# How the rows of graphs 1 to 3 are picked: by one-hot products on TensorE, or by transfers with an index

## What is computed

```python
x = x + tanh(g_xattn[0]) * xattn(ctx_512, layernorm(x))    # two gat layers, 8 heads of 32
x = x + tanh(g_ffn[0]) * ffn(layernorm(x))                 # top 2 of 8 experts
# gat layer: e = leaky_relu(a_self[i] + a_neigh[j]) - 1e10 * (1 - adj[i, j]); out = softmax(e) @ feat + b; elu
```

## Time and profile before

| | |
|---|---|
| time, median of 3 runs | 93.64 us (93.17 to 95.05) |
| time of the profiled execution | 93.16 us |
| its span, first to last instruction | 91.4 us |
| PE busy | 83.3 us (91%), 615 matmuls |
| DVE, ACT, POOL busy | 64.7, 55.2, 43.5 us |
| mean granted clock of PE | 0.996 |
| DMA | 5.44 MB; 386 to 405 GB/s from 6.9 to 13.7 us |

### The profile page before, as it was taken

One profiled execution on the slowest core, in us unless ns is written; L12 is line 12 of the kernel. 1 busy time (PEld: TensorE's weight loads), 2 busy tenths in 40 slices (PEclk: granted clock), 3 DMA queues, 4 the chain that ended last, 5 costly groups with the idle time before them and its releaser, 6 DMA issues.

```text
span 91.4 us, 1958 instructions
## 1 busy us (share of the span) xinstructions
PE 83.3 (91%) x615; PEld 78.1 (85%) x615; DVE 64.7 (71%) x202; ACT 55.2 (60%) x132; POOL 43.5 (48%) x95
## 2 busy tenths in 40 slices
PE   4959999989999999999999999999999999999800
PEld 4728888869899999989998999999999999999700
DVE  5887797857897609998599368795359767899520
ACT  1446888596695948398927799763366564433100
POOL 7970953698003999925900002885002988800000
PEclk9999999999999999999999999999999999999998
DMA  1999991000000000000000000030000030003021
GB/s 34 286 273 400 405 386 60 0 0 0 7 4 0 0 0 0 7 0 4 0 0 0 7 0 0 4 115 4 7 0 0 0 115 0 0 7 115 4 84 56
DMA packets 3339, 5.44 MB, mean 60 GB/s; under 512 B 474, under 2 KB 2748, under 8 KB 3068
## 3 DMA queue, kind: packets, MB, share of 16 engines
q1 hardware_dynamic: 3164, 5.00, 16.0%
q10 hardware_dynamic: 160, 0.26, 1.1%
HBM read 4.21 MB, written 1.05 MB: 58 GB/s over the span
## 4 chain that ended last, share of the span: by engine, by line
PE 59%; DVE 17%; DMA 6%; issue 6%; ACT 5%; DVEq 1%; POOL 1%; ACTq 1%
PE bank L734 6%; DMA ctx_sb<-in_ctx_t 6%; PE bank L735 6%; PE bank L739 6%; PE bank L896 6%; PE bank L781 5%; PE bank L872 5%; PE bank L783 5%; PE bank L782 5%; DVE hid_lo L1093 4%; PE bank L859 3%; PE bank L756 3%; DVE hid L1085 2%; PE bank L679 2%; DVE stat L990 2%
## 5 line engine op out<-in xcount | busy, mean ns | idle before, releaser
L1085 DVE TENSOR_TENSOR hid<-act_sb,bank 128x256 f32<-128x256 f32 x32 | 13.4, 418 | 10.9 <-PE bank L756 9.0
L518 ACT ACTIVATE act_sb<-bank,small_sb 128x256 f32<-128x256 f32 x32 | 15.1, 471 | 8.7 <-PE bank L739 8.4
L526 ACT CAST hid_hi<-hid 128x256 fp32r<-128x256 f32 x32 | 13.0, 405 | 10.7 <-DVE hid L1085 9.7
L781 PE MATMUL bank<-wdown_hi,hid_hi 128*128 128x256 f32 x64 | 18.4, 287 | 0.3 <-ACT hid_hi L526 0.3
L734 PE MATMUL bank<-xt_hi,wup_hi 128*128 128x256 f32 x64 | 18.0, 304 | 0.1
L783 PE MATMUL bank<-wdown_hi,hid_lo 128*128 128x256 f32 x64 | 18.1, 282 | 0.0
L782 PE MATMUL bank<-wdown_lo,hid_hi 128*128 128x256 f32 x64 | 18.0, 281 | 0.0
L735 PE MATMUL bank<-xt_hi,wup_lo 128*128 128x256 f32 x64 | 16.6, 281 | 0.0
L1093 DVE TENSOR_TENSOR hid_lo<-hid,hid_hi 128x256 fp32r<-128x256 f32 x32 | 13.4, 420 | 0.2
L739 PE MATMUL bank<-xt_lo,wup_hi 128*128 128x256 f32 x64 | 12.7, 280 | 0.0
L734 PEld LDWEIGHTS bank<-xt_hi,wup_hi 128*128 128x128 f32 x64 | 12.1, 189 | 0.5 <-ACT act_sb L518 0.3
(11 more groups left out here) (147 smaller groups left out, 180.6 us busy)
## 6 DMA issues: line engine op xcount, KB each, us to landing
x_sb<-in_x SPq DMA_DIRECT2D x4, 256.0 KB, 5.1
wup_sb<-in_wup SPq DMA_DIRECT2D x1, 1024.0 KB, 7.2
wdown_sb<-in_wdown SPq DMA_DIRECT2D x1, 1024.0 KB, 9.4
out<-out_sb SPq DMA_DIRECT2D x3, 256.0 KB, 2.2
check_sb<-in_check_w SPq DMA_DIRECT2D x1, 320.0 KB
w_sb<-in_w SPq DMA_DIRECT2D x1, 256.0 KB, 5.5
out<-out_sb SPq DMA_DIRECT2D x2, 128.0 KB, 2.5
ctx_sb<-in_ctx_t ACTq DMA_DIRECT2D x1, 192.0 KB, 5.6
```

The costliest lines, as they stand in the source:

```text
L518: nc.scalar.activation(act_out(n), bank[:, UP[n % 2], 0:N], ACT.Silu, bias=bup_sb[:, k % E:k % E + 1]).then_inc(silu_rdy, 1)
L526: nc.scalar.copy(hid_hi[:, n % HID_SLOTS, :], hid[:, n % 2, :]).then_inc(hid_hi_rdy, 1)
L781: nc.tensor.matmul(dst, hid_hi[:, n % HID_SLOTS, part], wdown_hi[:, e, :], start=False, stop=False, skip_group_check=True)
L1085: nc.vector.tensor_tensor(hid[:, n % 2, :], act_out(n), bank[:, PICK[n % 2], 0:N], ALU.mult).then_inc(hid_rdy, 1)
```

## The change

Graph 0 stays as it was. For graphs 1 to 3 the one-hot matrices, their transposes and squares and the products with z go. In their place:

- DVE writes for each row the number of its leader (`rows_leader`, `max_index`) into `leader`, 8 numbers a row, of which the first is used.
- SP stores `leader` of each graph to HBM, and later z of each graph. These six stores stand in SP's list behind all the loads.
- POOL (`leaders`) waits for the store and issues for each half graph a transfer that takes row leader(i) of the stored list into `leader2`: the leader of the leader. `fetch` takes row leader2(i) of the stored z into `rows`. Two transfers of 128 rows each for each graph: twelve in all. They stand among POOL's other work, `leaders(1)` ahead of `wup_part(0)`, `leaders(2)` ahead of `row_power(0)`.
- `gated` of graphs 1 to 3 waits for `rows_ld` and reads SBUF. On DVE `gated(1)` moves into step 0 of the expert loop, `gated(2)` to step 4, `gated(3)` to step 7. `wup_part(3)` on POOL moves ahead of `row_power(1)`.
- On PE `feat1(2, 1)` moves ahead of the transposes of graph 0. Some banks and the waits that guard them change.

```diff
-        onehot = sb("onehot", [P, NT, N], BF16)
-        onehot_t = sb("onehot_t", [P, B, C, N], BF16)
+        onehot = sb("onehot", [P, C, N], BF16)
+        onehot_t = sb("onehot_t", [P, C, N], BF16)
         source = sb("source", [P, C, N])
-        source_next = sb("source_next", [P, B - 1, C, N])
+        leader = sb("leader", [P, NT, 8], U32)
+        leader2 = sb("leader2", [P, NT, 8], U32)
+        rows = sb("rows", [P, B - 1, C, N])
+        leader_hbm = [nc.dram_tensor(f"leader_hbm{b}", [N, 8], U32) for b in range(1, B)]
...
+
+            for b in range(1, B):
+                sp.wait_ge(leader_rdy, C * b)
+                sp.dma_start(leader_hbm[b - 1][:].rearrange("(c p) k -> p c k", p=P), leader[:, pair(b), :]).then_inc(leader_st[b - 1], 16)
+            for b in range(1, B):
+                sp.wait_ge(z_rdy, b + 1)
+                sp.dma_start(z_hbm[b - 1][:].rearrange("(c p) d -> p c d", p=P), elu_exp[:, b, :, :]).then_inc(z_st[b - 1], 16)
...
-            def rows_onehot(b):
+            def leaders(b):
+                pool.wait_ge(leader_st[b - 1], 16)
                 for t in range(C * b, C * b + C):
-                    pool.wait_ge(top_rdy, t + 1)
-                    nc.gpsimd.tensor_scalar(onehot[:, t, :], x_sb[:, t, :], top[:, t, 0:1], None,
-                                            ALU.is_equal).then_inc(onehot2_rdy, 1)
+                    nc.gpsimd.indirect_dma_start(leader2[:, t, :], None, leader_hbm[b - 1][:],
+                                                 bass.IndirectOffsetOnAxis(leader[:, t, 0:1], 0)).then_inc(leader2_ld[b - 1], 16)
+
+            def fetch(b):
+                pool.wait_ge(leader2_ld[b - 1], 16 * C)
+                pool.wait_ge(z_st[b - 1], 16)
+                for t in range(C):
+                    nc.gpsimd.indirect_dma_start(rows[:, b - 1, t, :], None, z_hbm[b - 1][:],
+                                                 bass.IndirectOffsetOnAxis(leader2[:, C * b + t, 0:1], 0)).then_inc(rows_ld[b - 1], 16)
 
-            rows_onehot(1)
-            rows_onehot(2)
...
+            leaders(1)
             wup_part(0)
+            leaders(2)
             row_power(pool, 0, 0)
-            rows_onehot(3)
+            leaders(3)
             wup_part(1)
+            fetch(1)
             wup_part(2)
+            fetch(2)
+            wup_part(3)
             row_power(pool, 0, 1)
-            wup_part(3)
+            fetch(3)
             wdown_part(0)
             wdown_part(1)
             row_power(pool, 0, 2)
+            for b in range(1, B):
+                pool.wait_ge(rows_ld[b - 1], 16 * C)
...
-            turned(1)
...
-            source_copy(1)
...
-            source_copy(2)
...
-            act_experts(act, 0, {0: [lambda: source_copy(3)], 1: [lambda: wdown_part(0)],
+            act_experts(act, 0, {1: [lambda: wdown_part(0)],
                                  3: [lambda: wdown_part(1)], 5: [lambda: wdown_part(2)], 7: [lambda: wdown_part(3)]})
...
             if n == 1:
-                pe.wait_ge(z_rdy, B)
+                pe.wait_ge(z_rdy, 2)
...
-                pe.wait_ge(xa_rdy, C * (3 + nb))
+                pe.wait_ge(z_rdy, B - nb)
...
-            turn(0)
+            turn()
             feat1(0, 0)
             feat1(0, 1)
-            twice_part(0)
+            twice()
             feat0(3)
-            turn(1)
             feat1(1, 0)
-            gather(0)
-            twice_part(1)
+            gather()
             feat1(1, 1)
-            turn(2)
             feat1(2, 0)
-            twice_part(2)
+            feat1(2, 1)
             pe_xt(pe, 0, 0)
-            feat1(2, 1)
-            turn(3)
             feat1(3, 0)
             pe_gate(pe, 0, 0)
             feat1(3, 1)
-            twice_part(3)
-            gather(1)
-
-            pe_experts(pe, 0, {1: [lambda: gather(2)], 4: [lambda: gather(3)]})
+
+            pe_experts(pe, 0, {})
...
+            def rows_leader(b):
+
+                for t in range(C * b, C * b + C):
+                    dve.wait_ge(top_rdy, t + 1)
+                    nc.vector.max_index(leader[:, t, :], top[:, t, :], x_sb[:, t, :]).then_inc(leader_rdy, 1)
...
-                    dve.wait_ge(gather_mm, C + b)
-                    nc.vector.scalar_tensor_tensor(out=xa[:, pair(b), :], in0=both(GATHER[b][0]), scalar=gates[:, 0:1],
+                    dve.wait_ge(rows_ld[b - 1], 16 * C)
+                    nc.vector.scalar_tensor_tensor(out=xa[:, pair(b), :], in0=rows[:, b - 1, :, :], scalar=gates[:, 0:1],
                                                    in1=x_sb[:, pair(b), :], op0=ALU.mult, op1=ALU.add).then_inc(xa_rdy, C)
...
             elu0(0)
             rows_top(1)
+            rows_leader(1)
             elu0(1)
...
             elu1(0)
+            rows_leader(2)
+            elu0(3)
             rows_top(3)
-            elu0(3)
             gated(0)
             dve_stats(dve, 0, 0)
-            turned(2)
+            rows_leader(3)
...
-            turned(3)
...
-            gated(1)
-            dve_stats(dve, 0, 1)
...
-            dve_experts(dve, 0, {0: [lambda: gated(2), lambda: dve_stats(dve, 0, 2)], 
-                                 5: [lambda: gated(3), lambda: dve_stats(dve, 0, 3)], 13: [check_peaks],
+            dve_experts(dve, 0, {0: [lambda: gated(1), lambda: dve_stats(dve, 0, 1)],
+                                 4: [lambda: gated(2), lambda: dve_stats(dve, 0, 2)],
+                                 7: [lambda: gated(3), lambda: dve_stats(dve, 0, 3)], 13: [check_peaks],
                                  2 * E + 3: [check_peak_max], 2 * E + 5: [check_peaks_all], STEPS + 6: [check_flag]})
```

More of the change, by code:

```diff
@@ L563, in bias_part, with turned @@
                 nc.scalar.copy(bias_parts[:], bias_sb[:]).then_inc(bias_hi_rdy, 1)
[L565 to L571, removed]
+            def turned():
+                act.wait_ge(turn_mm, 1)
+                nc.scalar.copy(onehot_t[:], turned_bank()).then_inc(onehot_t_rdy, 1)
             def minus0(b):
@@ L603, in _ @@
             exp0(1)
-            turned(0)
+            turned()
             minus0(2)
@@ L817, in _, with turn, twice @@
         def _(pe):
[L818 to L827, removed]
+            def turn():
+                pe.wait_ge(ident_bf_rdy, 1)
+                pe.wait_ge(onehot_rdy, C)
                 for i in range(C):
                     for j in range(C):
-                        mm = nc.tensor.transpose(turned_bank(b)[:, j, i * P:(i + 1) * P],
-                                                 onehot[:, C * b + i, j * P:(j + 1) * P], ident_bf[:])
+                        mm = nc.tensor.transpose(turned_bank()[:, j, i * P:(i + 1) * P],
+                                                 onehot[:, i, j * P:(j + 1) * P], ident_bf[:])
                 mm.then_inc(turn_mm, 1)
-            def twice_part(b):
-                if b == 1:
-                    pe.wait_ge(source0_rdy, 1)
-                if b == 2:
-                    pe.wait_ge(h1_rdy, B)
-                if b < 2:
-                    pe.wait_ge(onehot_t_rdy, b + 1)
-                else:
-                    pe.wait_ge(onehot_t2_rdy, b - 1)
+            def twice():
+                pe.wait_ge(onehot_t_rdy, 1)
                 for j in range(C):
                     for k in range(C):
-                        mm = nc.tensor.matmul(both(TWICE[b])[:, j, :], onehot[:, C * b + k, j * P:(j + 1) * P], onehot_t[:, b, k, :],
+                        mm = nc.tensor.matmul(both(TWICE)[:, j, :], onehot[:, k, j * P:(j + 1) * P], onehot_t[:, k, :],
                                               start=(k == 0), stop=(k == C - 1))
@@ L878, in feat1, with gather @@
                     mm.then_inc(feat1_mm, 1)
-            def gather(b):
-                if b == 0:
-                    pe.wait_ge(h1_rdy, 3)
-                if b == 1:
-                    pe.wait_ge(z_rdy, 3)
-                if b == 0:
-                    pe.wait_ge(source0_rdy, 1)
-                else:
-                    pe.wait_ge(source_rdy, b)
-                pe.wait_ge(z_rdy, b + 1)
+            def gather():
+                pe.wait_ge(h1_rdy, 3)
+                pe.wait_ge(source_rdy, 1)
+                pe.wait_ge(z_rdy, 1)
                 for t in range(C):
-                    dst = bank[:, GATHER[b][t], t * D:(t + 1) * D]
-                    rows = slice(t * P, (t + 1) * P)
+                    dst = bank[:, GATHER[t], t * D:(t + 1) * D]
                     for j in range(C):
-                        hot = source[:, j, rows] if b == 0 else source_next[:, b - 1, j, rows]
-                        mm = nc.tensor.matmul(dst, hot, elu_exp[:, b, j, :], start=(j == 0), stop=(j == C - 1))
-                    if b == 0 or t == C - 1:
-                        mm.then_inc(gather_mm, 1)
+                        mm = nc.tensor.matmul(dst, source[:, j, t * P:(t + 1) * P], elu_exp[:, 0, j, :], start=(j == 0), stop=(j == C - 1))
+                    mm.then_inc(gather_mm, 1)
             pe.wait_ge(warm_rdy, 1)
```

(11 more changed lines are left out.)

29 lines of the change are left out of this document (12 added, 17 removed).

## The result

The changed kernel takes 102.22 us (median of 4 runs, 101.69 to 103.01), the kernel before, on the same chip, 93.41 us (4 runs): a ratio of 1.095, 95% interval 1.088 to 1.101. The forecast was 99.0 with a range of 94.5 to 104.5. The profiled execution took 101.69 us, with a span of 99.9; the one before took 93.16 with a span of 91.4. Some executions of a kernel are over 1.5% longer than its fastest one, and the ratios leave those out.

The account below looks back on a forecast made before the run. The prediction took VectorE's arrival at the first `hid`, then PE, as the bound: 93.16 + 4.9 (first `hid` later, through POOL's transfers) + 0.9 (clock) = 99.0 us, eight in ten from 94.5 to 104.5.

Parts of the forecast that it names:

- What bounds the kernel: VectorE's chain to the first `hid` (38.2 us), then PE to the end; a delay there passes on one for one.
- What is removed: Ahead of 33.2 us, PE loses 7.2 us and POOL 5.7; counts only as far as VectorE's chain starts sooner.
- rival (d): PE's 7.2 us are the gain, 86 to 87 us; needs first `hid` by 32 against a 37.9 floor; chance 0.02.
- The price of a transfer, c: POOL's own time for each indirect transfer of 128 rows, taken as 1.1 us, between 0.4 and 1.7.
- Rival (a): POOL transfers are cheap, c = 0.4: first `hid` at 38 to 39.4, time 93 to 94.3 us; chance 0.09.
- rival (c): POOL's transfer price is high, 1.7 us: +10.1, 103 to 104 us; chance 0.27 shared with (b).
- (b): POOL and VectorE hold each other up, 0.41 us per transfer on ten: +4.1, 103 us; 0.27 shared with rival (c).
- When the first store lands: Graph 1's leaders, queued on SP behind the loads, land at 16.2 us, one microsecond behind the last load.
- Graph 0's shift: `row_power(0)` on POOL, behind `leaders(1)`, `wup_lo` and `leaders(2)`: ready at 22.9 us instead of 18.2, 4.7 late.
- `row_power(1)`: On POOL behind ten transfers: ends at 35.1 us, including a 0.8 us wait for z(1); VectorE ready sooner, at 33.7.
- Behind it: From `row_power(1)` through ScalarE, `score_t` and two gates with statistics, 8.0 us to the first `hid` at 43.1, +4.9.
- Clock: PE's clock falls in its pause ahead of graph 0's transposes; two sets of four transposes double: +0.9 us.

Follow-up runs that it names:

- experiment 4: Changed kernel with each of the six `leaders` transfers issued a second time into a tile nobody reads; 108.57 us, ratio 1.158.
- experiment 3: Changed kernel with the picking left out: plain SP loads bring the stored rows back, no POOL transfers by index; 93.3 us, ratio 0.999.
- experiment 6: Changed kernel with POOL's `wdown_part(0)` and `(1)` moved behind `row_power(2)`; 102.38 us, ratio 1.099.
- experiment 5: Experiment 3 with `gated(2)`, `gated(3)` and their statistics moved to steps 8 and 12, `scores(1)` ahead of `row_power(3)`; 94.21 us, ratio 1.011.
- 9: Experiment 5 with `check_peaks` (six reductions on VectorE) split and moved behind the 7th `hid`; 93.34 us, ratio 1.000.
- experiment 7: Changed kernel with graph 1's leaders stored from ScalarE's queue, behind `exp0(2)`, instead of SP's; 102.27 us, ratio 1.089.
- experiment 1: Changed kernel with `wup_part(0)` and `row_power(0)` moved ahead of `leaders(1)` on POOL; 100.81 us, ratio 1.081.
- experiment 2: Changed kernel with 46 unused matmuls on PE ahead of graph 0's transposes; 102.54 us, ratio 1.100.
- experiment 8: Changed kernel with POOL reordered for graph 1 first, low parts of `wdown` and `bdown` on VectorE, later gates; 99.25 to 101.38 us against 93.26.

## Why the prediction was right, point by point

**What bounds the kernel: right in the main, not one for one.** The change gives +7.9 at the first `hid` and +8.5 at the end, experiment 4 gives +6.4 and 5.9 to 6.35, experiment 3 gives 0 and 0. But each of these moves POOL's whole list, and with it the scores of graph 1 as well as the first `hid`, so they don't tell the two apart. Where the first `hid` moves and the 7th doesn't follow, nothing passes: 0.9 us earlier (experiment 6) and 3.3 us earlier (experiment 5) were worth nothing. What passes one for one is the 7th `hid`, 38.5 us ahead of the last matmul in every kernel with this order. In experiment 5 VectorE has all the work of graphs 2 and 3 still to do before it. The prediction asked only about a delay.

**What is removed: right.** PE's 7.2 us are worth nothing by themselves. Experiment 3 has them gone and takes the time of before, and its first `hid` at 38.25 is close to the floor of 37.9 that was worked out against rival (d). In experiment 3 as in 9, 3.5 us of the 7.2 turn into waits of PE between 24 and 32 us.

**The price of a transfer, c: 1.1 against 1.25.** That is the mis-sized term: 0.95 busy plus 0.30 issue. Over the ten transfers ahead of `row_power(1)` it is 1.5 us of the 3.0 by which the first `hid` was later than forecast (46.1 against 43.1). Rival (a), which needed c under 0.6, and rival (c), 1.7, are out. The measured 102.22 lies in the forecast's range and in the band of 102 to 107 that (b) and (c) shared; c and the slip of 7.9 are what speak for the forecast. The low end of the range is loose: a slip of 1.9 at c = 0.6 gives 95.1, not 94.5.

**When the first store lands: 16.2 against 15.68.** The time was right. The prediction gave SP's order of issue as the reason. It was issued at 10.12 without a delay, and experiment 7 shows the landing to be the same from an empty queue. It lands just behind the loads (5 GB/s in 15.0 to 15.3 us, nothing after) whichever queue it is on. That the DMA engines' load as such holds it is what is left, not shown by itself; the prediction took it as the time and not as the cause.

**Graph 0's shift: 22.9 against 23.17**, 4.95 late instead of 4.7, with everything that was named as waiting behind it. But it isn't a term of the sum by itself: experiment 1 takes 3.6 us out of it, and the first `hid` doesn't move. The prediction did sum over POOL's whole list and not over this pause, and that is why it came out near.

**`row_power(1)`: 35.1 against 37.06.** The 10 x 0.15 for c, and 0.43 and 0.20 of waits on POOL for `wup_hi` and VectorE, less 0.5 for the store; and the last `wup_lo` took 1.67 instead of 1.28 while `gated(1)` ran beside it. VectorE, expected ready at 33.7, was ready only at 35.9. Two things lie on its path: the low clock under graph 0's pieces of PE, and the 1.36 us by which `ldiff` was held. POOL waited only 0.20 for it, so either list alone gives nearly the same end.

**Behind it: 8.0 against 9.0.** The sign of being right that named the first `hid` at 43 to 44 failed: 46.09. The 1.34 us by which `gated(2)` was held are more than the difference. The prediction had the lock as rival (b), on transfers, with 0.41 each. No transfer was held (eleven of the twelve take 0.94 to 1.03, the first 1.23). It was VectorE that waited, for POOL's subtractions, as `nmean` did before. Whether it also waits for the transfers is not separated: `ldiff` began at 29.89, 0.22 us before the subtraction, inside the span of a transfer. Rival (b)'s time, 103, came near for another reason than its own.

**Clock: +0.9 forecast.** The size is near, by other pieces. The four transposes of graph 0 took 0.46 more, those of graph 1 ran at 1.00 again, and the four matmuls behind the first took 1.71 instead of 0.86. From graph 0's shift to the first `hid` it is 22.9 us, and 22.1 in experiment 2, where the clock is 1.00 up to 32 us: about 0.8.

So the forecast's 99.0 for the profiled 101.7 was short by 1.5 for c, about 1.3 for the lock, and 0.6 behind the first `hid`; the 0.9 for the clock, added beside the slip, lies within the measured 7.9. The mechanism was right and the sizes of two terms were not. That they were small enough for the range is in part luck: nothing in the sum had the lock at `gated(2)`.

## What to carry to other kernels

Before work is moved from a busy engine to an idle one's queue, add up the receiving queue ahead of its next instruction on the critical path: here twelve instructions of 1.25 us on an engine that had been 48% busy cost 8.8 us, and 7.2 us less on PE were worth none. Saved time counts only if the chain that sets the next stage starts sooner, and then only until the next full engine; experiments 5 and 9 lost the gain to VectorE and to PE in turn. Whether it helps to put short, awaited items first in a list is not shown here: experiment 1 did it for one item and the first `hid` didn't move, and in experiment 8 it brought two engines side by side that hold each other up.

## What the runs showed of the hardware

- A transfer by index of 128 rows costs POOL 0.95 us and 0.30 of issue whether a row is 32 bytes (`leader`) or 1 KB (`rows`). The first of a run took 1.23. From issue to landing it is 2.4 us for `leader` and 2.8 for `rows`, so the time on POOL can't be read from the landing.
- A store of 8 KB, issued while the loads run, took 5.56 us from SP and 4.35 from ScalarE's empty queue; both landed at 15.7.
- While POOL subtracts (two inputs in SBUF), some VectorE instructions stand until it is done: `ldiff` 1.52 instead of 0.16, `score` with 16 columns 3.40 instead of 0.17, `gated(2)` 2.08 instead of 0.74. `gated` had its first input in PSUM before and has both in SBUF now. By the Trainium skill (SBUF — State Buffer, "Who interferes with whom") a VectorE instruction with two inputs in SBUF contends with a GpSimd instruction that reads SBUF, and the one that issued first keeps the shared ports for its whole length; the trace and experiment 6 agree that VectorE stands until POOL is done. On who came first they agree for `gated(2)`, which began 1.0 us behind POOL's pair, and for the last `wup_lo`, which began 0.22 behind `gated(1)` and took 1.67 instead of 1.28. `ldiff` and `score` began 0.22 and 0.50 ahead of the subtraction, while POOL was at a transfer, and were held all the same. Instructions with one input are held too: `nmean` 1.26 before the change, and in experiment 8 the copy of `wg_parts` 1.25 instead of 0.17. That VectorE's form of `gated` brought the lock with it is argued from this, and was not tried with the input left in PSUM.
- The clock fell to 0.50 in a pause of PE from 18.2 to 23.95 us. It was still 0.50 in each stretch of 2 us from 24 to 32, with PE busy 2.00 of 2.00 in each, and 0.92 in 32 to 34. Filling one pause moved the fall to a later one (experiment 2).
